# Row statistics moved from the self attention stage to the first stage; two products of the last stage as three products of rounded halves

## The reference, cut to what matters

```python
x = x + cross_attention_16_heads(layernorm(x), ctx)              # first stage
u = layernorm(x); nx = layernorm(u, ln1_w, ln1_b)                # double norm
y = u + self_attention(nx)                                       # self attention stage
x = x + y + moe(layernorm(y, ln2_w, ln2_b))                      # routed there, experts next
out = softmax(q @ k.T / 8) @ v ; x = x + out @ Wo + bo           # last stage, 8 heads of 64
xn = layernorm(x)                                                # last stage, norm_f
scale = max(|xn| in blocks of 32) / 7.5 ; q6 = nearest_fp6(xn / scale)
x = x + (q6 * scale) @ dequantised(weight).T + bias              # "quantised rows' product"
```

## Time and profile before

| | |
|---|---|
| median of three runs | 2076.18 us |
| the profiled execution's own time | 2077.91 us |
| its span | 2076.1 us (1.8 us lie around it) |
| PE busy | 1971.5 us, 95% |
| DVE, ACT, POOL busy | 1356.3, 1082.9, 924.2 us |

### The profile page before, as it was taken

One profiled execution on the slowest core, in us unless ns is written; L12 is line 12 of the kernel. 1 busy time (PEld: TensorE's weight loads), 2 busy tenths in 40 slices (PEclk: granted clock), 3 DMA queues, 4 the chain that ended last, 5 costly groups with the idle time before them and its releaser, 6 DMA issues.

```text
span 2076.1 us, 59362 instructions
## 1 busy us (share of the span) xinstructions
PE 1971.5 (95%) x20383; PEld 1636.4 (79%) x20384; DVE 1356.3 (65%) x3358; ACT 1082.9 (52%) x2530; POOL 924.2 (45%) x1554
## 2 busy tenths in 40 slices
PE   7999999998889999799999999889999999999995
PEld 5888888886677777599999999767777778778784
DVE  6777777775488888643333333348878788787875
ACT  2555555554467777332222332356666666666672
POOL 4544545452377777500000000256666666666651
PEclk9999999999799999899999999979999999999998
DMA  8232232330440000211111111311111111110100
GB/s 224 85 100 93 86 108 83 110 86 2 164 159 27 22 22 24 83 33 35 35 38 38 35 35 35 98 29 29 33 30 40 28 38 32 35 35 28 40 19 9
DMA packets 98072, 118.73 MB, mean 57 GB/s; under 512 B 9442, under 2 KB 90466, under 8 KB 97890
## 3 DMA queue, kind: packets, MB, share of 16 engines
q1 hardware_dynamic: 91874, 103.32, 16.2%
q0 software_dynamic: 6144, 14.69, 2.4%
HBM read 67.26 MB, written 50.72 MB: 57 GB/s over the span
## 4 chain that ended last, share of the span: by engine, by line
PE 84%; DVE 6%; issue 5%; ACT 2%; POOL 1%; DMA 1%; DVEq 0%; POOLq 0%; ACTq 0%; SPq 0%
PE ps_proj L258 19%; PE ps_quad L1433 11%; PE ps_out L1448 10%; PE ps_quad L578 5%; PE ps_quad L136 4%; PE ps_out L158 4%; PE ps_turned L147 4%; PE ps_out L586 3%; PE ps_proj L1863 3%; PE ps_proj L1842 3%; DVE s_negmax L1030 2%; PE ps_proj L662 2%; PE ps_turned L564 2%; PE ps_out L1202 1%; PE ps_proj L1152 1%
## 5 line engine op out<-in xcount | busy, mean ns | idle before, releaser
L1352 ACT ACTIVATE e_act_T<-ps_quad,fc_b 128x128 f32<-128x128 f32 x504 | 137.2, 384 | 313.3 <-PE ps_quad L1433 313.3
L1433 PEld LDWEIGHTS ps_quad<-e_xT,e_w_now 128*128 128x128 f32 x2016 | 234.6, 192 | 7.7 <-DVE e_xT L1392 3.9
L1433 PE MATMUL ps_quad<-e_xT,e_w_now 128*128 128x128 f32 x2016 | 235.7, 275 | 3.4 <-DVE e_xT L1392 3.4
L1448 PE MATMUL ps_out<-w,e_act_T 128*128 x1008 | 228.1, 379 | 0.8 <-DVE e_y L1400 0.8
L413 ACT ACTIVATE a_probsT<-ps_quad 125x1792 f32<-125x1792 f32 x96 | 160.0, 1666 | 101.5 <-PE ps_quad L578 101.5
L1448 PEld LDWEIGHTS ps_out<-w,e_act_T 128*128 128x128 f32 x1008 | 186.6, 190 | 24.0 <-issue 1.2
L1581 POOL MEMSET c_cT<- 128x2 f32 x2 | 0.1, 102 | 461.0 <-DMA c_wk<-in_L_xattn_Wk 461.0
L1389 DVE COPY e_w_now<-w 128x2048 f32 (+1 forms) x63 | 77.3, 1227 | 191.8 <-PE ps_quad L1433 188.5
L1577 POOL TENSOR_TENSOR c_kL<-c_kT,c_kH 128x376 fp32r<-128x376 f32 x128 | 126.3, 987 | 155.1 <-ACT c_kH L1646 154.4
L178 DVE TENSOR_SCALAR c_probs<-c_probs,c_recip 112x375 f32<-112x375 f32 x256 | 155.9, 649 | 4.6
L1641 ACT ACTIVATE c_kT<-ps_proj 128x376 f32<-128x376 f32 x128 | 62.0, 484 | 175.6 <-PE ps_proj L258 175.6
(11 more groups left out here) (316 smaller groups left out, 5375.2 us busy)
## 6 DMA issues: line engine op xcount, KB each, us to landing
slots<-a_zeros SPq DMA_DIRECT2D x60, 512.0 KB, 5.0
a_cT<-in_ctx_t SPq DMA_DIRECT2D x32, 375.0 KB, 3.6
c_cT<-in_ctx_t SPq DMA_DIRECT2D x32, 375.0 KB, 3.2
w<-in_fc_t SPq DMA_DIRECT2D x2, 4096.0 KB, 19.3
w<-in_fc_t SPq DMA_DIRECT2D x8, 1024.0 KB, 12.2
e_xg<-slots SPq DMA_DIRECT2D x63, 128.0 KB, 2.0
slots<-e_y SPq DMA_DIRECT2D x63, 128.0 KB, 1.7
out<-c_fo SPq DMA_DIRECT2D x32, 112.0 KB, 1.9
```

The costliest lines, as they stand in the source:

```text
L1352: last = act.activation(act_T[par][:, c * TILE:(c + 1) * TILE], hidden[par][:, c // 4, (c % 4) * TILE:(c % 4 + 1) * TILE], ACT.Gelu, bias= ...
L1433: last = pe.matmul(hidden[par][:, c // 4, (c % 4) * TILE:(c % 4 + 1) * TILE], w1_now[:, k, c * 128:(c + 1) * 128], xT[par][:, k, :], start ...
L1448: last = pe.matmul(y_ps[:, 0:D], act_T[1 - par][:, c * TILE:(c + 1) * TILE], w2[:, bass.ds(e, 1), c, :].rearrange("p a d -> p (a d)"), sta ...
```

## The change

The statistics of the residual rows and `double_norm` go from the self attention stage to the first stage, one batch behind the residual sum. In the last stage oT and xdT, and the two weights once, are split into rounded halves; the products become chains of three fp32r terms (12 and 6 instructions); the quantised rows' product moves one batch back (b-3), which adds a step at the end; the loop's written-out steps grow from `1, 2` to `1, 3, 4`.

```diff
 # cross_first: POOL, end of step b
+                    if exists(b - 1):
+                        double_norm(b - 1)
 # cross_first: POOL, before its steps: five small memsets, one wait (as in self_attention before)
 # cross_first: DVE, between the statistics of b+3 and k_split(later, par, 1)
+                    if exists(b - 1):
+                        dve.wait_ge(x_ready, b)
+                        wait(dve, rates_ready, b - 1)
+                        norm_u.dve_moments(dve, b - 1, row(residual, b - 1))
 # self_attention: POOL
-                    if exists(ahead):
-                        double_norm(ahead)
 # self_attention: DVE, first in the step
-                    if exists(ahead):
-                        wait(dve, rates_ready, ahead)
-                        norm_u.dve_moments(dve, ahead, row(residual, ahead))
 # cross_last: POOL, between context_high and qL
+                    if exists(b - 3):
+                        pool.wait_ge(xd_high, b - 2)
+                        pool.tensor_tensor(xdL[1 - par][:, :, :], xdT[1 - par][:, :, :], xdH[1 - par][:, :, :], ALU.subtract).then_inc(xd_low, 1)
+                    if exists(b - 1):
+                        pool.wait_ge(o_high, b)
+                        pool.tensor_tensor(oL[:, :, :], oT[:, :, :], oH[:, :, :], ALU.subtract).then_inc(o_low, 1)
 # cross_last: ACT, part 2, behind the copy of oT
+                            act.wait_ge(o_ready, b)
+                            act.activation(oH[:, :, :], oT[:, :, :], ACT.Copy).then_inc(o_high, 1)
 # cross_last: ACT, part 3, behind the copy of xdT
+                            act.wait_ge(xdT_ready, b - 1)
+                            wait(act, f_mm, b - 3)
+                            act.activation(xdH[par][:, :, :], xdT[par][:, :, :], ACT.Copy).then_inc(xd_high, 1)
 # cross_last: ACT, end of step 0; DVE, start of step 1
+                        act.activation(woH[:, :, :], wo[:, :, :], ACT.Copy)
+                        act.activation(wfH[:, :, :], mem["wf_t"][:, :, :], ACT.Copy).then_inc(wo_high, 1)
+                        dve.tensor_tensor(woL[:, :, :], wo[:, :, :], woH[:, :, :], ALU.subtract)
+                        dve.tensor_tensor(wfL[:, :, :], mem["wf_t"][:, :, :], wfH[:, :, :], ALU.subtract).then_inc(wo_split, 1)
 # cross_last: PE, part 3
-                            pe.wait_ge(o_ready, b)
-                            for k in range(4):
-                                last = pe.matmul(proj[0:T, 0:D], oT[:, k, :], wo[:, k, :], start=(k == 0), stop=(k == 3))
+                            pe.wait_ge(o_low, b)
+                            chain(pe, proj[0:T, 0:D], [term for k in range(4) for term in split_terms((oH[:, k, :], oL[:, k, :]), (woH[:, k, :], woL[:, k, :]))])\
+                                .then_inc(op_mm, 1)
-                        if exists(b - 2):
-                            pe.wait_ge(xdT_ready, b - 1)
-                            for k in range(2):
-                                last = pe.matmul(proj[0:T, D:2 * D], xdT[:, k, :], mem["wf_t"][:, k, :], start=(k == 0), stop=(k == 1))
+                        if exists(b - 3):
+                            pe.wait_ge(xd_low, b - 2)
+                            chain(pe, proj[0:T, D:2 * D], [term for k in range(2) for term in split_terms((xdH[of][:, k, :], xdL[of][:, k, :]), (wfH[:, k, :], wfL[:, k, :]))])\
+                                .then_inc(f_mm, 1)
-                over_batches(pe, step, 1, 2)
+                over_batches(pe, step, 1, 3, 4)      # the same on SP, POOL, ACT and DVE
```

More of the change, by code:

```diff
@@ L376, in k_low, with double_norm @@
                     pool.tensor_tensor(kL[to][:, t, :], kT[:, t, :], kH[to][:, t, :], ALU.subtract).then_inc(k_ready, 1)
+                def double_norm(b):
+                    pool.wait_ge(norm_u.moments_ready, 2 * b + 2)
+                    mean, var = norm_u.moments[:, 0:1], norm_u.moments[:, 1:2]
+                    pool.tensor_tensor(u_minus[:, :], zero[:, :], mean, ALU.subtract)
+                    pool.tensor_tensor(u_spread[:, :], var.to_broadcast([T, 2]), var_scale[:, :], ALU.mult).then_inc(u_step, 1)
+                    pool.wait_ge(u_step, U_STEP * b + 1)
+                    pool.tensor_tensor(u_spread[:, :], u_spread[:, :], var_add[:, :], ALU.add).then_inc(u_step, 1)
+                    pool.wait_ge(u_step, U_STEP * b + 2)
+                    pool.tensor_tensor(row(rates, b), u_spread[:, :], mem["minus_half"][0:T, :].to_broadcast([T, 2]), ALU.pow).then_inc(u_step, 1)
+                    pool.wait_ge(u_step, U_STEP * b + 3)
+                    pool.tensor_tensor(row(shifts, b), u_minus[:, :].to_broadcast([T, 2]), row(rates, b), ALU.mult).then_inc(rates_ready, 1)
                 def step(b, par):
@@ L806, in _ @@
                 pool.wait_ge(mem["slots_cleared"], 32 * (NB - 2))
[L808 to L820, removed]
                 def out_norm(b, par):
@@ L1484, in cross_last @@
         xn, xq, xd = sb("xn", [T, D]), sb("xq", [T, D]), sb("xd", [T, D])
-        xT, xdT = sb("xT", [128, 2, T]), sb("xdT", [128, 2, T])
+        xT, xdT = sb("xT", [128, 2, T]), [sb(f"xdT{i}", [128, 2, T]) for i in range(2)]
+        xdH, xdL = ([sb(f"xd{n}{i}", [128, 2, T], F32R) for i in range(2)] for n in "HL")
         qT, kT = sb("qT", [128, 4, T]), sb("kT", [128, 4, CTXE])
@@ L1619, in step @@
                         context_low(later, par)
[L1620 to L1623 removed]
+                    if exists(b - 3):
+                        pool.wait_ge(f_biased, b - 2)
+                        wait(pool, f_out[1 - par], 8 * (b - 4 + par))
+                        pool.tensor_tensor(fo[1 - par][:, :], f[:, :], row(residual, b - 3), ALU.add).then_inc(f_ready, 1)
                     if exists(b - 1):
                         norm_f.pool_rstd(pool, b - 1)
[L1627 removed]
+                over_batches(pool, step, 1, 3, 4)
             @block.scalar
@@ L1826, in step @@
                             wait(pe, o_biased, b - 1)
-                            wait(pe, f_biased, b - 2)
+                            wait(pe, f_biased, b - 3)
                             k_product(b, par, 2)
@@ L1896, in program @@
         residual = sb("residual", [T, NB, D])
+        mem["rates"], mem["shifts"], mem["rates_ready"] = sb("rates", [T, NB, 2]), sb("shifts", [T, NB, 2]), sem("rates_ready")
         first = cross_first(nc, mem, ctx_t, w, residual)
```

75 lines of the change are left out of this document (42 added, 33 removed).

## The result

The kernel after took 2059.66 us (median of 4 runs, 2055.24 to 2061.87), the kernel before 2076.30 beside it (4 runs): ratio 0.9916, 95% interval 0.9899 to 0.9934. The forecast was 2058. The profiled execution after took 2059.53, its span 2057.7. The total came out; the next table shows that its parts did not. Each row is the change of one stretch, from the two profiled executions; the anchors are first starts of the same instruction in both.

The account below looks back on a forecast made before the run. PE was taken to bound the first and last stages, a DVE, PE and POOL loop self attention. Terms -10.8 - 1.6 - 8.4 + 1.8 + 1 = -18.0 us gave a median of 2058 us, range 2045 to 2070.

Parts of the forecast that it names:

- Self attention steps, -10.8: Self attention: moving DVE's statistics out shortens each step by 0.40 us, 9.85 to 9.45, over 27 steps: -10.8 us.
- Rival B: Both stages reach PE's floor: self attention gains 17.5 us, last stage 15.3; time 2044 us; chance 0.12.
- rival C: Self attention gains 0.1 us or less a step, since POOL's DMA issue and k_high set the loop; 2066 us; chance 0.08.
- The turn, -1.6: Turn from first stage to self attention: first rates ready early, so PE's L1226 comes at 522.8, not 524.50: 1.6 us gained.
- First stage, 0: First stage: the moved DVE and POOL work is hidden in idle time, DVE with 0.3 us left: cost 0.
- Rival E: First stage: the insert makes L522 and PE's maxima scores 0.2 us late, +6 us; 2064 us; chance 0.06.
- The two products: Last stage: chains of 12 and 6 take PE 2.26 us instead of 2.77, 0.51 saved; net -0.28 a step, -8.4 us.
- Stall (a): Last stage: oH on ACT delays the k copy, so PE idles 0.23 us ahead of q projection L1842 each step.
- (b): Last stage: POOL's oL is ready at 1743.35, PE reaches the output product at 1743.64: no wait, by 0.3 us.
- DVE's slide of up to 1.8 us: Last stage: behind POOL's xdL and oL, second L178, mixing and statistics slide into DVE's 2.84 us idle ahead of L1756.
- Rival A: Last stage gains nothing: DVE instructions get in around xdL, each holding POOL about 0.25 us; 2066 us; chance 0.15.
- The tail, +1.8, with +1 for more written-out steps: Program end: later quantised rows' product adds 2.2 us, shorter output product returns 0.4; two more written-out steps at each end, +1.

Follow-up runs that it names:

- e1: Kernel before with only double_norm and its row statistics moved to the first stage, last-stage products as before: 2115.9 us, 0.9969 of before.
- e2: Kernel before with only the last stage's products of rounded halves, statistics where they were: 2121.07 us, 0.9999 of before.
- a1: The whole change run again, same code as the kernel after, on another chip: 2127.9 us, 1.0017 of before.
- e3: Kernel after with oH formed on ACT behind the copy of k, ahead of the exponentials: 2107.21 us, 0.9926 of before.
- e4: Kernel after with oH formed on ACT behind the exponentials and the copy of probsT: 2131.04 us, 1.0041 of before.
- e7: Kernel after with only the output product in halves, quantised rows' product one float32 product, oH behind the copy of k: 2116.0 us, 0.9980 of before.
- e5: Kernel after with POOL's two self attention scatters moved behind its products q and k_high: 2104.12 us, 0.9919 of before.
- e8: Kernel after with scatters behind k_high, oH behind the copy of k, and the copy of n2 behind out_norm: 2079.36 us, 0.9790 of before.

## Why the prediction was right, and where it was not

The total was right by luck: two errors of over 4 us, self attention's steps (-4.8) and the second half (+4.4), had opposite signs, and two shifts of the clock (-2.1 and +2.7) nearly cancelled.

**Self attention steps, -10.8: the mechanism was right, the size too small.** Where before takes 2076 us, the step's term "I take 0.40, 0.46 at most" counted only DVE's gap between the output rows' end and their statistics. After, that gap is 0.13 us, not 0.61:

```profile
709.43 0.65 DVE L1079 SCALAR_TENSOR_TENSOR s_y_rows<-residual,rates,s_o 112x256 f32<-112x256 f32 x1 [0.16 <-DVE s_o L1076]
...
710.21 0.43 DVE L231 BATCH_NORM_STATS2 s_norm_o_stats<-s_y_rows 112x6 f32<-112x256 f32 x1
...
710.95 2.02 DVE L1036 TENSOR_REDUCE s_negmax<-ps_quad 112x16 f32<-112x1792 f32 x1
```

That is 0.48 us. "The rest of the loop keeps its length" failed: from the end of the maximum to the end of k_high it took 5.99 us (703.80 to 709.79) after 6.16 before, and from the statistics to the maximum 0.74 after 0.78. Together 0.69, enough to pass under PE's row of 9.28 us; what the step gained is 9.83 - 9.28 = 0.55, and between 0.6 and 1.3 in each of the four steps ahead of those (the fifth to the eighth), 0.96 in the mean. "Leaving out double_norm frees POOL without moving this part" was right within 0.17: POOL's idle time in front of the slots is now 1.7 to 2.0 us. Rival B was right for this stage. In the sets at 2121 us rival C was, through the hold by the scatter. That the moved work made these steps shorter is shown, for nothing else changed in this stage; that it was DVE's gap and not POOL's row is read from these rows, and no run tested it where before takes 2076.

**The turn, -1.6:** -1.7 measured (3.76 us of PE idle before), and -0.5 before it. Right. What came behind it, 2.1 us between the first maximum and the first mask product at 0.95 instead of 0.50 of the clock, was in no step of the prediction. e1 and after had it, the profile of before not; e2, without the moved statistics, had it too (4.7 us), and a1, the same code as after, had not (6.9 us): this gain is chance, and not the change's.

**First stage, 0:** right. DVE's idle time ahead of q fell from 1.04 to 0.37 us (27.1 and 9.7 us over 26 waits each, 100 to 500 us), near the 0.3 that was forecast, and the stage ended 0.5 us sooner. Rival E fell.

**The two products.** Chains of 12 and 6 take 2.30 us against 2.26 forecast. Stall (a), 0.23 us: found, at its place (0.2 us, 19 of 19 steps), and confirmed by e3, which takes it away: 0.17 us less than after, 0.23 less than e2, 0.35 less than a1. (b), "no wait, by 0.3 us": right, 0.4 us, and e4 shows the price past it. DVE's slide of up to 1.8 us into its idle time: 1.9. In the step shown a waiting DVE instruction did not get in between xdL and oL (1721.49 + 0.65, then 1722.11); so it is in 29 of after's 32 steps, where oL takes 1.12 us. In the other 3, and in 11 of e3's 32, it does get in and costs POOL little: in e3's rows above both L178 end at 1771.83, before oL does, with xdL at 0.76 and oL at 1.24 us. The Trainium skill ("SBUF — State Buffer", section "Who interferes with whom") says that the order of issue decides which of the two engines blocks; the traces show both outcomes of the same code, and the prediction's rule from the earlier trace rows, that DVE waits for the last of a row, holds for most steps only. Rival A fell all the same, since a DVE instruction let in cost 0.1 us and not 0.25, and oL had 0.4 to spare.

Yet the step gained 0.17, not 0.28. Start to start, in the mean of 25 steps, the products take 2.30 us and not 2.77 (-0.47, forecast -0.51), PE's turns ahead of the q projection 0.86 and not 0.65 (the stall, +0.21), and the q projection itself 1.97 and not 1.88 (+0.09, in no step of the prediction). That is the 0.17. The q projection's 0.09 comes with the stall: in e3, which has no stall, it is 1.88 again (lengths of 2.04 and 1.95 in the rows).

**The tail, +1.8, with +1 for more written-out steps:** +4.1 measured, in two places. Behind the last bias sum it is +2.7 (21.3, was 18.6; e7, with the old order of that product, has 18.6 again). The step's sum of the two rounds through PE, DVE and POOL was 4.7 us, of which the rows above show 5.2 (2045.50 to 2050.7: the chains take 1.6 each at the lower clock, not 1.3), against 2.5: sized 0.5 too low. The other place was taken for a gain: "the shorter output product in the step before gives 0.4 back". It does (PE's chain 3.85 us, after 3.21 + 1.08), but DVE's rounding sets that step, and two of its instructions now take about 1.3 us each, next to xdL and to oL on POOL. The chain of waits of after, POOL beside it, then the chain of before:

```profile
2024.02 1.32 DVE c_probs L178
...
2030.01 1.30 DVE c_mx_q L1273
...
2032.44 3.85 PE ps_proj L258 x18
```

```profile
2024.48 0.65 POOL L1625 TENSOR_TENSOR c_xdL<-c_xdT,c_xdH 128x224 fp32r<-128x224 f32 x1
2029.89 1.13 POOL L1628 TENSOR_TENSOR c_oL<-c_oT,c_oH 128x448 fp32r<-128x448 f32 x1 [4.76 <-ACT c_oH L1693]
```

```profile
2051.77 0.44 DVE c_mx_q L1267
...
2053.12 3.21 PE ps_proj L1863 x8
```

From the bias sum to xd it takes 9.98 us, was 8.36; the step 14.6, was 13.2. DVE's slide costs nothing in the steady steps, where it has idle time, and is in full view here. The step of the prediction that failed is the one that looked at this part of the tail for PE's products alone. The "+1" for more written-out steps no run shows by itself; the tail's two places make up the 4.1 without it.

Sum of the second half without the clock: -5.3 + 4.1 = -1.2 where -5.6 was forecast. e2 measured it by itself, before at 2121 us: 0.9999.

**What stays open.** Why three sets ran with steps of 10 to 13 us in self attention: the hold is placed (it ends 2.7 to 2.8 us after the first scatter's start, in e1, e3, e5 and e8), not explained; the run that would have taken the scatters away fell on a chip at 2076 us. Since each chip showed one of the two times only, whether it is a property of the chip was not tested either. And what sets whether the clock rises 8, 12 or 15 us after the last stage's first maximum.

## What to carry to other kernels

When one engine's instruction is moved into another's queue, its worth hangs on the place in the queue by tenths of a microsecond: oH one place too early cost 0.23 us a step and ate over half of what the products gain (0.42 us a step from e1 to e3, 0.19 from e1 to e2); one place too late it cost 0.67. Read for each place both who waits behind it and who waits for it, and put it where the later of the two still has time. A software pipeline made one batch deeper, and work that only idle time hides, have their price at the end, where nothing hides them: count every engine's turns there, in queue order. And measure the halves of a change apart: run apart, before at 2121 us, they gave 0.9969 and 0.9999, and where before takes 2076 the stretches put nearly all of the gain into the first half.

## What the runs showed of the hardware

The kernel before ran 45 us (2.2%) apart in two sets, the kernel after 68 us (2059.66 and 2127.9). Of a1's 68.5 us of span over after, 66.4 had arisen when the last stage began: 3.2 ahead of the first mask product, 62.7 in the self attention steps. The first three steps, which have no scatter, took 9.0 to 9.4 us in both. In the sets at 2121 us an instruction of DVE or ACT that waited for PE, or PE's own signalling matmul, started 2.7 to 2.8 us after the first scatter did, which is about when that scatter lands in before and after (2.65 us). The scatters themselves are no slower there: the last packet of the two ends 3.56 us after the first scatter's start in before, after, e1, a1 and e8 alike (medians of 15 to 19 pairs). The traces of these sets record no landing for any of the 64 scatters, those of before and after for all. A ratio measured where before takes 2076 (0.9916) did not hold where it takes 2121 (1.0017).

The last stage's first 21 us had a granted clock of 0.81 or 0.82 in before, e1, e3 and a1, of 0.72 in e4 and of 0.64 in after and e2, with PE busy 17.9 to 19.7 us in them; the first bias sum came 43, 44 and 46 us after the first maximum. Kernels with the products stand on both sides, a1 and after are even the same code, so up to 3 us of a difference between two single profiles may be this alone.
